# Cross-scan layers: side products of an image finish and of the next softplus at other tiles of a turn

## What is computed

```python
def step(h, inp):
    dt, ut, bt, ct = inp
    dA = jnp.exp(dt[..., None] * A_k[None])
    dBu = dt[..., None] * bt[:, :, None, :] * ut[..., None]
    h = dA * h + dBu
    y = jnp.einsum('bkdn,bkn->bkd', h, ct)
    return (h, y)
...
delta = jax.nn.softplus(delta + delta_bias[None, :, None])
...
y4 = (y4 - mu) / jnp.sqrt(var + EPS)
y4 = out_norm_weight[None, :, None, None] * y4 + out_norm_bias[None, :, None, None]
y = jnp.transpose(y4, (0, 2, 3, 1))
y = y * jax.nn.silu(z)
return jnp.einsum('bhwd,cd->bhwc', y, out_proj_weight)
```

## Time and profile before

| | us |
|---|---|
| median of three runs | 4379.65 |
| the profiled execution | 4376.48 |
| its span | 4374.7 |
| VectorE busy | 3388.8 (77%) |
| TensorE busy | 2973.8 (68%), mean granted clock 0.729 |
| GpSimd busy | 2301.3 (53%) |
| ScalarE busy | 2027.5 (46%) |

### The profile page before, as it was taken

One profiled execution on the slowest core, in us unless ns is written; L12 is line 12 of the kernel. 1 busy time (PEld: TensorE's weight loads), 2 busy tenths in 40 slices (PEclk: granted clock), 3 DMA queues, 4 the chain that ended last, 5 costly groups with the idle time before them and its releaser, 6 DMA issues. The chain is left out here.

```text
span 4374.7 us, 26874 instructions
## 1 busy us (share of the span) xinstructions
PE 2973.8 (68%) x5896; PEld 691.0 (16%) x5896; DVE 3388.8 (77%) x2145; ACT 2027.5 (46%) x2238; POOL 2301.3 (53%) x984
## 2 busy tenths in 40 slices
PE   3768778777777860055555555467877877777786
PEld 1111111111111110011111111111111111111111
DVE  1799899989989937855455555179999999998992
ACT  2466565555656620032323232246646656465662
POOL 0587676757757720013131313057767676775872
PEclk9678786787777855576767676567868778778785
DMA  1554645536545420010101010155464563654642
GB/s 38 125 134 124 152 110 139 142 99 159 128 117 135 113 62 14 4 29 0 29 0 29 0 29 0 35 121 139 118 149 118 132 145 97 156 132 109 148 114 61
DMA packets 127572, 402.78 MB, mean 92 GB/s; under 512 B 29783, under 2 KB 30685, under 8 KB 127117
## 3 DMA queue, kind: packets, MB, share of 16 engines
q1 hardware_dynamic: 127436, 401.47, 38.2%
HBM read 273.98 MB, written 6.29 MB: 64 GB/s over the span
## 5 line engine op out<-in xcount | busy, mean ns | idle before, releaser
L1243 POOL TENSOR_TENSOR L_read<-L_state,L_c_rows 128x1024 f32<-128x1024 f32 x768 | 1807.9, 2363 | 748.7 <-DVE L_state L1335 622.9
L1335 DVE TENSOR_TENSOR_SCAN L_state<-L_decay,L_b_ps 128x1024 f32<-128x1024 f32 x768 | 1756.0, 2286 | 28.4 <-DVE L_b_ps L1320 2.1
L1061 PE MATMUL L_y_ps<-L_read,L_fold 128*64 128x512 f32 x3072 | 1294.5, 936 | 437.0 <-POOL L_read L1243 420.0
L1183 ACT ACTIVATE L_decay<-L_delta,L_a_neg 128x1024 f32<-128x1024 f32 x768 | 877.7, 1146 | 551.2 <-DVE L_state L1335 547.8
L1320 DVE TENSOR_TENSOR L_b_ps<-L_du,L_b_ps 128x1024 f32<-128x1024 f32 x768 | 937.6, 1221 | 235.9 <-issue 201.6
L600 POOL TENSOR_TENSOR L_read<-L_state,L_c_rows 128x1024 f32<-128x1024 f32 x96 | 225.6, 2350 | 831.7 <-DVE L_state L705 831.7
L1173 ACT COPY L_b_ps<-L_b_rows 128x1024 f32<-128x1024 f32 x256 | 260.3, 1017 | 407.6 <-DVE L_state L1335 295.0
L1061 PEld LDWEIGHTS L_y_ps<-L_read,L_fold 128*64 128x64 f32 x3072 | 188.1, 165 | 1408.5 <-POOL L_read L1243 1080.8
L1041 PE MATMUL L_side_ps<-g_cm,L_w_u 96*128 (+1 forms) x216 | 185.9, 951 | 92.2 <-DVE L_cent_w L1289 36.7
L559 ACT ACTIVATE L_decay<-L_delta,L_a_neg 128x1024 f32<-128x1024 f32 x96 | 110.3, 1149 | 281.8 <-DVE L_state L705 239.0
L1041 PE MATMUL L_side_ps<-L_dbl,L_w_dt 128*128 128x512 f32 x216 | 179.9, 928 | 87.3 <-ACT L_delta L1110 85.8
(11 more groups left out here) (236 smaller groups left out, 2935.9 us busy)
## 6 DMA issues: line engine op xcount, KB each, us to landing
L_c_rows<-L_bc_dram SPq DMA_DIRECT2D x516, 256.0 KB, 4.0
L_b_rows<-L_bc_dram SPq DMA_DIRECT2D x516, 256.0 KB, 4.2
L_delta<-L_delta SPq DMA_DIRECT2D x228, 256.0 KB, 5.4
L_du<-L_du SPq DMA_DIRECT2D x164, 256.0 KB, 5.9
L_du<-L_u SPq DMA_DIRECT2D x64, 256.0 KB, 5.8
L_bc_dram<-L_dbl SPq DMA_DIRECT2D x36, 128.0 KB, 3.4
x_cm<-in_x SPq DMA_DIRECT2D x1, 1536.0 KB, 8.6
out_y<-x_cm SPq DMA_DIRECT2D x1, 1536.0 KB, 7.1
```

What stands on the lines that cost most here:

```text
L1061: m = nc.tensor.matmul(y_ps[i * BLK:(i + 1) * BLK, c, :], fold[:, :], y_half(t, o, i), start=first, stop=last, skip_group_check=True)
L1183: nc.scalar.activation(decay[:, t % DECAYS, :], delta2[:, d * NBLK + c, :], ACT.Exp, scale=a_neg[:, o * 2 + d, c, p:p + 1]).then_inc(decay ...
L1243: nc.gpsimd.tensor_tensor(read[:, t % READS, :], state[:, t % STATES, :], c_rows[:, g % 2, :], ALU.mult).then_inc(multiplied, 1)
L1335: nc.vector.tensor_tensor_scan(state[:, t % STATES, way], decay[:, t % DECAYS, way], fed[:, way], 0.0, ALU.mult, ALU.add).then_inc(scanned, 1)
```

## The change

- SOFTPLUS_TURN of the r = 0 turns goes from tile 22 to 28, so all dt and sum products, ACT's and POOL's softplus steps move by six tiles there.
- In finishing turns shift, cent, var and out move from tiles 7 to 23 to tiles 12 to 30; silu from 8 to 11, the root from 24 to 30, POOL's addition to x from 26 to 34. z and the copy of y stay.
- DVE takes its side products three tiles after PE's tile instead of two.
- u and bc of the r = 0 turns move among each other.
- COPY_ABOVE goes from groups 12 to 14 to groups 13 to 15, in all turns.
- In the head ACT's softplus steps of the three blocks are interleaved, and POOL's gap and du steps likewise.

```diff
-ACT_LAG, DVE_LAG = 4, 2
+ACT_LAG, DVE_LAG = 4, 3
-FINISH = {("z", 0): (0, 1), ("z", 1): (2, 3), ("shift", 0): (7, 8), ("cent", 0): (9, 11), ("cent", 1): (13, 15),
-          ("var", 0): (19, 20), ("out", 0): (21, 23)}
-SOFTPLUS_TURN = (22, 17)
-PREPARE = [{("u", 0): (5, 6), ("u", 1): (10, 12), ("u", 2): (14, 16), ("bc", 0): (17, 18)},
+FINISH = {("z", 0): (0, 1), ("z", 1): (2, 3), ("shift", 0): (12, 14), ("cent", 0): (17, 19), ("cent", 1): (21, 23),
+          ("var", 0): (25, 26), ("out", 0): (28, 30)}
+SOFTPLUS_TURN = (28, 17)
+PREPARE = [{("u", 0): (5, 6), ("u", 1): (8, 9), ("bc", 0): (10, 11), ("u", 2): (13, 15)},
            {("u", 0): (4, 5), ("u", 1): (7, 8), ("bc", 0): (10, 11), ("u", 2): (13, 14)}]
-SILU_AT, RSTD_AT, Y_AT, ADD_AT = 8, 24, 3, 26
+SILU_AT, RSTD_AT, Y_AT, ADD_AT = 11, 30, 3, 34
 SKIP_AT = (1, 2, 3)
-COPY_BELOW, COPY_ABOVE = (1, 2, 3), (12, 13, 14)
+COPY_BELOW, COPY_ABOVE = (1, 2, 3), (13, 14, 15)
...
+            ahead = {0: (("exp", 0), ("log", 0), ("one", 0), ("less", 0), ("exp", 1), ("log", 1), ("relu", 0), ("one", 1),
+                         ("less", 1)),
+                     1: (("exp", 2), ("log", 2), ("relu", 1), ("one", 2), ("less", 2)), 2: (("relu", 2),)}
             for _, key, i in HEAD_SIDES:
                 if key[0] == "sum" and i == 0:
-                    for kind in ("exp", "log", "one", "less", "relu"):
-                        softplus(Head(), kind, key[1])
+                    for kind, j in ahead[key[1]]:
+                        softplus(Head(), kind, j)
                 take(Head(), key, i)
...
-            for j in range(NJ):
-                softplus(Head(), "gap", j)
-                softplus(Head(), "du", j)
+            for kind, j in (("gap", 0), ("gap", 1), ("du", 0), ("gap", 2), ("du", 1), ("du", 2)):
+                softplus(Head(), kind, j)
```

## The result

The changed kernel takes 4414.23 us (median of four runs, 4411.83 to 4418.63) against 4381.09 us of the kernel before, run beside it (four runs, 4374.66 to 4390.14). The ratio is 1.0079, with a 95% interval of 1.0067 to 1.0091: slower by 0.8%, about where the forecast put it. The profiled execution took 4411.83 us, its span is 4410.1, the mean granted clock 0.731.

A forecast was written before the change was run, and what follows sets the result against it. DVE (VectorE) was taken to set the pace throughout the two cross-scan layers. Profiled 4376.5 - 22.8 (heads) - 18 (finishing turns) + 75 (boundaries) = 4410.7 us, 4413.9 on the median's footing; predicted 4414, range 4375 to 4460.

The forecast's parts named there:

- The boundaries: Turn boundaries: third copy behind next turn's loads delays product 48, 6.9 us eight times and 3.3 six times, 75 us lost.
- The finishing turns: Six turns that also finish an image: side-product waits fall from 15.0 to 12.0 us each, 18 us gained in all.
- The heads: Two layer heads: interleaved softplus takes 11.4 us of ScalarE's time off each, 22.8 us gained.
- The odd turns: Plain turns: longer by the boundary wait of 3.3 or 6.9 us and nothing else.
- (a): Rival, 18 in 100: boundary chain paid, but turns save 9 us and copies land in 5.2; 4358 to 4378 us.
- (b): Rival, 6 in 100: copies issued in group 15 are covered, so boundaries cost nothing; 4339 to 4303 us.
- (c): Rival, 12 in 100: landings at 8.7, ACT's lateness at 6.5 and no gain in the turns; 4476 us.
- low end: Fast edge of the range: landings at 5.2 and turns at 7 saved, 4375 us.
- part 3: Turn boundaries: COPY_ABOVE one group later makes the first decay wait for delta's third copy, 75 us lost.
- My estimate of 3 us for a landing: Boundary copies: whole landing in 3 us would make part 3 cost some 26 us, sum 0.3% below before.

The follow-up runs named there:

- Copies_only: Kernel before with only COPY_ABOVE moved, from groups 12 to 14 to groups 13 to 15: 4428.97 us, ratio 1.0127.
- Add_33b: Changed kernel with ADD_AT 33 instead of 34, GpSimd's addition to x ahead of gap 0: 4399.64 us, ratio 1.0040 to the kernel before.
- out_27b: Changed kernel with the out products at PE tiles 27 and 29 instead of 28 and 30: 4373.40 us, ratio 0.9991 to the kernel before.
- head_only: Kernel before with only the head's new order on ACT and GpSimd: 4348.39 us, ratio 0.9946.
- third_14: Changed kernel with COPY_ABOVE (13, 14, 14), the third copy back in group 14: 4377.19 us, ratio 1.0004 to the kernel before.
- b_first: third_14 with the load of B's row ahead of C's in group 15: 4347.68 us, ratio 0.9934 to the kernel before.
- q1_aheadb: b_first with the second copy issued between load_b and load_c in group 14: 4339.71 us, ratio 0.9915 to the kernel before.

## Why the prediction was right

The forecast of 4414 met the measured 4414.23, and that close it is luck: three terms were off by 15.4, 7.9 and 4.7 us, the first against the other two. What was right is the direction, the steps of the chain at the boundaries and the parts of the finishing turns.

**The boundaries.** The mechanism was right in each step: the third copy behind the loads of group 15, `load_c` waiting for read 44, the first decay waiting for a delta DMA, the copy of B behind it, DVE waiting for that. The size was 90.4 us in place of 75. The term that was too small is the chain's length. The issue time was right (3.7 us). The landing took 7.1 us, not 6.6, and 6.7 to 8.1 over all 14 boundaries: six transfers ahead of it at 1.2 us each set it, even from an empty queue. And read 44 ends 5.6 us behind scan 44, not 5.1. So product 48 came 18.65 us behind the end of scan 44 in place of 17.55: 1023.52 to 1042.17. That is 1.1 us per boundary, 8.8 over the eight even to odd ones; the odd to even ones came out 1.1 higher as well (4.4 in place of 3.3 each), 6.7 over six. Copies_only shows what the copies do by themselves: 71.5 us at the even to odd boundaries against 30.3 before. The step from there to 94.2 is the late read 44, which softplus brings. And the three versions that go from 94.2 by 76.6 and 60.2 to 39.3 us, with softplus where the change put it, show that the cost goes with these queue positions; 9.0 us of it are left in the last.

**What the prediction did not see** is the second chain. That ACT "is bound by the landing of B" in before was right, and it should have led on to: with softplus six tiles later, the copies move later too and `load_c` with them, so B's row is late even if the copies are not. It had no effect on the forecast, as the third copy came last anyway, but undoing only COPY_ABOVE 15 gave 33 us less than I then expected.

**The finishing turns.** -18.6 in place of -18, and the parts are those of the sum. In the turn shown: `shift` 1.17 (0.8 predicted), `cent` 0, the first `out` 2.81 (2.8 predicted, from the earlier trace rows), the second 3.31 (3.8), tile 39 3.44 (4.5). That is 10.7 where the sum had 11.9, and three small waits for the copy of B that I had not priced (0.71 + 0.51 + 0.74 = 2.0) bring it to 12.7. Add_33b and out_27b each took one cause away and found its effect at its tiles (17.4 us at tile 39; 29.9 at tiles 30 to 33). So the mechanisms are shown, and the agreement to 0.6 us over six turns is in part two small errors against each other. In one turn of layer 3 (turn 2) the `shift` tile still took 9.1 us; the other five are at 4.0 to 5.4. Add_33b has one such turn too, another one; what sets them apart isn't settled.

**The heads.** -30.7 in place of -22.8. The ACT steps were right (11.4 each), but I held TensorE's products at their old duration. It came to 17.7 us in layer 0 and 13.0 in layer 3. Of the 7.9 us on top, 4.6 are sum 2 behind its shorter pause, which every version with the new order shows; 3.8 are sums 0 and 1 in layer 0 at a granted clock of 1.00, which head_only did not have (0.91), so they belong to the execution and not surely to the edit; and sum 1 of layer 3 took 0.5 more than before.

**The odd turns** gave 4.7 us, where I had said "nothing else": a stall of 1.1 us at tile 30 that seven of the eight had before and two after. What makes it and why it went isn't settled; copies_only, where only the boundaries moved, has it in three turns.

**The rivals.** (a) needed the small waits to vanish and copies that land in 5.2: the small waits did not vanish. (b) is refuted at its own point: the copy would have had to land 2.2 us before product 48 is due, and ACT waits 11.0 us for it. (c) fell on the turns, which gained. One slip in the range: its low end charges the boundaries with 60 us, where landings of 5.2 give 55, so it should have been 4370 and not 4375. The rule of the Trainium skill that I set beside part 3 ("DMA: Bandwidth & Descriptors", section "Rules for kernel authors": issue early, wait late) points the right way in all four versions that move a DMA (copies_only later and slower, third_14, b_first and q1_aheadb earlier and faster). My estimate of 3 us for a landing, from that page's fixed cost, which it gives for DMAs that GpSimd issues, does hold for a copy that SP issues into an empty queue. In the head of layer 0 of the changed kernel the first copy of delta goes out at 103.91, with nothing under way, and its landing is

```profile
DMA to landing us min/median/max: 3.0/3.0/3.0
```

It does not hold at the boundary, where the same kind of copy took 7.1 us with six transfers ahead of it. What was wrong was to reckon it without the queue, and the earlier trace rows, whose 4.6 us I set against it, have a pair of loads ahead of them.

## What to carry to other kernels

When side work moves by some tiles, follow its DMAs in the queue as well: they went past one load that waits for a slow engine, and 0.8% was lost while both intended parts gained. A resource that several producers share in order (here the one side bank) should be asked for a tile ahead of the next user, not in the same tile behind it: that was worth 41 us here for two numbers. And after undoing the last cause of a wait look for the one that was hidden under it; here it took three steps (the copy, B's row behind C's, the copy ahead of both) until the boundary was nearly free (4.9 us in place of 3.8).

## What the runs showed of the hardware

In the heads, a pair of 128x512 matmuls took 2.07 to 2.08 us behind a pause of 8.4 us (four heads, of the kernel before and copies_only) and 1.12 to 1.13 behind one of 1.6 (the sixteen heads of the versions with the new order). Behind 3.7 us, in the same sixteen, it took 2.07 to 2.08 in twelve, 1.88 in one and 1.12 in three, all three of layer 0. So the same head can find the granted clock at 0.91 in one execution and 1.00 in another, and TensorE's 36 instructions there at 22.09 or 18.40 us: a gain of some us in such a stretch isn't the edit's until other executions show it too.

A 256 KB copy from SBUF to SBUF landed 3.0 us after its issue with nothing under way, 4.6 to 5.8 with one pair of loads ahead, 5.9 to 7.1 behind four row loads, and 6.4 to 7.5 there in the version with the copies alone. Transfers issued close behind each other land about 1.2 us apart, so its place in the queue at the boundary is worth 1.3 us in the landing on top of its own later issue.
